# A windowed attention block on one core: the score correction moves from a stage of its own into the loop over columns

## What is computed

```
x = x + attention(layer_norm_over_channels(x))
t = tokens(x)                      # 1600 tokens of 128
t = t + mixture_of_experts(layer_norm(t))   # 8 experts, top 2, 128 -> 128 -> 128, gelu
```

```
qkv = xt @ w_qkv.T + b_qkv
q = q * 16 ** -0.5
k_w = unfold(k).reshape(B, K2, C, L)...     # the flat (channel, offset) axis read as (offset, channel)
attn = softmax(einsum('bhnc,bhnlc->bhnl', q, k_w)) * mask
out = einsum('bhnl,bhnlc->bhnc', attn, v_w);  out = out @ w_proj.T + b_proj
```

## Time and profile before

| | us |
|---|---|
| median of 3 runs | 521.09 |
| lowest, highest | 521.02, 524.63 |
| the profiled execution's own time | 524.98 |
| its span in the profile | 523.2 |

### The profile page before, as it was taken

The page is one execution under the profiler, slowest core; times in us unless marked ns, Lnnn a source line. Parts: engine busy times, 40 slices in busy tenths (PEclk is TensorE's granted clock), DMA queues, the critical chain, the costliest instruction groups (busy, mean ns, idle before and its releaser), DMA issues.

```text
span 523.2 us, 15325 instructions
## 1 busy us (share of the span) xinstructions
PE 482.3 (92%) x6330; PEld 333.3 (64%) x6330; DVE 344.0 (66%) x841; ACT 315.1 (60%) x479; POOL 228.8 (44%) x312
## 2 busy tenths in 40 slices
PE   4999986789769999999999999999869999998996
PEld 1799964555346777677777676777645545685553
DVE  1201387865029999999999888898567745553453
ACT  2390099992299999998999988798400000242442
POOL 9100000100019989989999899999150000000011
PEclk9775599965569999999999999999999955869999
DMA  5078007510102566656666544555864000004600
GB/s 187 16 227 235 7 2 208 198 76 23 63 38 94 191 217 192 223 189 199 204 203 205 199 169 163 172 176 186 210 225 86 1 0 0 1 1 151 246 16 31
DMA packets 27618, 68.40 MB, mean 131 GB/s; under 512 B 8037, under 2 KB 14966, under 8 KB 26494
## 3 DMA queue, kind: packets, MB, share of 16 engines
q1 hardware_dynamic: 26686, 66.03, 39.4%
q0 software_dynamic: 144, 1.18, 0.6%
q10 hardware_dynamic: 720, 0.23, 0.2%
HBM read 37.83 MB, written 28.47 MB: 127 GB/s over the span
## 4 chain that ended last, share of the span: by engine, by line
PE 80%; ACT 9%; issue 6%; POOL 2%; DVE 1%; DMA 1%; SPq 0%; POOLq 0%; ACTq 0%; DVEq 0%
PE ps L776 17%; PE ps L844 10%; PE ps L799 8%; PE ps L816 7%; ACT slabs L584 6%; PE ps L781 5%; PE ps L754 4%; PE ps L883 4%; PE ps L711 3%; PE ps L903 3%; PE ps L704 3%; PE ps L802 3%; PE ps L741 2%; PE ps L664 2%; PE ps L856 1%
## 5 line engine op out<-in xcount | busy, mean ns | idle before, releaser
L776 PE MATMUL ps<-slabs 128*32 128x401 f32 x528 | 116.6, 510 | 4.3 <-issue 4.1
L776 PE MATMUL ps<-prb,slabs 128*32 128x401 f32 x494 | 112.8, 513 | 0.0
L1028 DVE CUSTOM_DVE_ANT_0 scn<-ps,con 128x401 f32<-128x401 f32 x120 | 64.9, 563 | 20.3 <-PE ps L781 20.0
L610 ACT ACTIVATE exb<-scn,lowest 128x401 f32<-128x401 f32 x120 | 74.1, 620 | 5.5 <-DVE lowest L1028 5.0
L456 POOL TENSOR_TENSOR slabs<-con,qrot 128x192 f32<-128x192 f32 (+4 forms) x67 | 32.7, 492 | 100.2 <-DMA kimg<-qrot 75.1
L456 POOL TENSOR_TENSOR slabs<-con,kimg 128x192 f32<-128x192 f32 (+4 forms) x63 | 76.1, 1214 | 0.0
L781 PEld LDWEIGHTS ps<-con,slabs 128*32 128x32 f32 x960 | 42.0, 111 | 47.7 <-issue 47.3
L1018 DVE COPY_PREDICATED slabs<-con,zt 128x1152 f32<-128x1152 int32 x41 | 64.2, 1565 | 8.4 <-ACT slabs L577 8.3
L462 POOL TENSOR_TENSOR slabs<-con,sbd 128x384 f32<-128x384 f32 x40 | 43.2, 1080 | 49.2 <-ACT sbd L599 49.2
L507 POOL TENSOR_TENSOR xln<-xln,wide 128x400 f32<-128x400 f32 x4 | 4.9, 1230 | 129.9 <-DVE wide L1176 129.9
L781 PE MATMUL ps<-con,slabs 128*32 128x128 f32 x960 | 59.3, 276 | 0.0
(11 more groups left out here) (138 smaller groups left out, 849.0 us busy)
## 6 DMA issues: line engine op xcount, KB each, us to landing
slabs<-zsl SPq DMA_DIRECT2D x40, 539.5 KB, 4.4
zsl<-uv SPq DMA_DIRECT2D x44, 484.5 KB, 3.2
slabs<-combd SPq DMA_DIRECT2D x2, 1600.0 KB, 8.5
skb<-zsl SPq DMA_DIRECT2D x4, 539.5 KB, 7.0
kimd<-kimg SPq DMA_DIRECT2D x1, 1612.0 KB, 6.7
vimd<-vimg SPq DMA_DIRECT2D x1, 1612.0 KB, 9.6
frd<-wide SPq DMA_DIRECT2D x2, 800.0 KB, 6.6
con<-ctab POOLq DMA_DIRECT2D x1, 1155.5 KB, 5.6
```

The source lines that it names most:

```text
L610: nc.scalar.activation(v(ex[x & 1], a, (1, NC3)), v(scn, (x & 1) * NB * NC3 + a, (1, NC3)), ACT.Exp, scale=-1.0, bias=lowest[:, NB * (x & ...
L776: mm(bank(g, (1, NC3), parts=TW, p0=TW * i), w, v((kt, kh)[b & 1][x & 1], b // 2 * C, (1, NC3)), start=first, stop=False, skip_group_check ...
L1028: nc.vector.tensor_tensor_reduce(v(scn, i * NC3, (1, NC3)), bank(g, (1, NC3)), cv("pos"), 1.0, 3e38, ALU.add, ALU.min, lowest[:, i:i + 1]) ...
```

## The change

The score correction is computed per chunk of 4 columns x (XC = 4, ten chunks). Chunk 0 is computed in front of the loop by DVE, chunks 1 to 9 in it: POOL multiplies (`boundary_mul`), DVE adds (`boundary_add`), each a quarter of a chunk per iteration. PE and ACT have no part in it.

- The queries are projected once in plain layout (4 products of 400 columns, `qn`), written to DRAM (`qd`) and read back per chunk, spread over 120 rows (`q_load`: 4, 4, 4 and 3 transfers for the four groups of components).
- The key image goes to DRAM column by column with its border (`kx`, copied by DVE), and is read back in two parts (`edges_in`); DVE takes the differences (`edge_difference`).
- The crossing probabilities are now taken by PE (12 products of 32x46 per column in turn_probs, table `edge_y`); DVE multiplies them with a mask out of PSUM and adds two halves. `pick` and `boundary_probs` are gone.
- `mask` is computed only for the 16 columns of EDGES (240 columns of elements instead of 160); the other 24 use the row mask of the constants directly.
- In front of the loop zslab order is 0, 1, 2, 3; the loop starts when slabs 0 and 1 are turned; zturn(2) and (3) stand behind scores(0), zt_copy(2) and (3) behind half_blocks(1). `vimg` goes to DRAM after the loads of chunk 1.

```diff
+GROUPS = ((0, 4), (4, 8), (8, 12), (12, 15))
+EDGES = [x for x in range(SZ) if x < PAD or x >= SZ - PAD]
-        ZORDER = (1, 2, 3, 0)
+        ZORDER = (0, 1, 2, 3)
...
@@ sync
+            def q_load(c, g):
+                if c == 0:
+                    sp.wait_ge(S["qb_zero"], 1)
+                    sp.wait_ge(S["qn_out"], 16)
+                else:
+                    sp.wait_ge(S["kmul"], 4 * (c - 1) + g + 1)
+                for cc in range(*GROUPS[g]):
+                    n = NCC - cc
+                    sp.dma_start(v(qb, cc * XE, (1, XE), parts=8 * n),
+                                 dv(qd, cc * L + c * XE, (0, n), (HC * L, 8), (1, XE))).then_inc(q_in[g], 16)
...
             load(1)
+            for g in range(len(GROUPS)):
+                q_load(1, g)
+            sp.wait_ge(S["v_copied"], NQ)
+            images_out(sp, vimg, vimd, S["vim_out"])
             for i in range(SZ):
                 if i + 2 < SZ:
                     store(i + 2)
+                if i == 0:
+                    q_load(2, 0)
+                c, g = divmod(i + 9, XC)
+                if c < NXC:
+                    q_load(c, g)
                 if 2 <= i:
                     load(i)
@@ gpsimd
             def boundary(x):
+                pool.wait_ge(S["kadd"], x // XC + 1)
...
+            def boundary_mul(c, g):
+                a, z = GROUPS[g]
+                pool.wait_ge(q_in[g], 16 * (z - a) * (c + 1))
+                if g < 3:
+                    pool.wait_ge(S["kadd_sum"], 4 * (c - 1) + max(g, 1))
+                else:
+                    pool.wait_ge(S["kadd"], c)
+                n = 8 * NCC
+                gp.tensor_tensor(v(kprod, a * XE, (XE, z - a), (1, XE), parts=n), v(qb, a * XE, (XE, z - a), (1, XE), parts=n),
+                                 v(dkx, (c * XC + a) * SZ, (SZ, z - a), (1, XE), parts=n), ALU.mult).then_inc(S["kmul"], 1)
...
             for i in range(SZ + 2):
                 if 2 <= i + 1 < SZ:
                     spread(i + 1)
                     boundary(i + 1)
                 if 2 <= i < SZ:
                     mask(i)
-                if 0 <= i - 2 < SZ:
-                    pick(i - 2)
+                c, g = divmod(i + 6, XC)
+                if (c, g) > (1, 1) and c < NXC:
+                    boundary_mul(c, g)
@@ scalar
             half_blocks(0)
+            slab(0)
+            slab(1)
             half_blocks(1)
+            zt_copy(2)
+            zt_copy(3)
@@ tensor, turn_probs
+                for g in range(NB):
+                    for i in range(NTW):
+                        last = mm(bank(7, (64, 2), (1, NR), off=128 + HC * g + 1, parts=TW, p0=TW * i),
+                                  v(ex[x & 1], g * NC3 + TW * i, (1, TW)), cv("edge_y", (1, 2 * NR), off=2 * NR * i),
+                                  start=(g == 0), stop=(g == NB - 1), skip_group_check=True)
@@ vector
+            def boundary_add(c, g):
+                dve.wait_ge(S["kmul"], 4 * c + g + 1)
+                a, z = GROUPS[g]
+                row = lambda r, n=2: v(kprod, r * XE, (1, n * XE), parts=8 * NCC)
+                acc = lambda n=2, o=0: v(kacc, o * XE, (1, n * XE), parts=8 * NCC)
+                if g < 3:
+                    tt(row(a), row(a), row(a + 2), ALU.add).then_inc(S["kadd_part"], 1)
+                    if g:
+                        dve.wait_ge(S["kadd_part"], 3 * c + g + 1)
+                        if g > 1:
+                            dve.wait_ge(S["kadd_sum"], 4 * c + g - 1)
+                        elif c:
+                            dve.wait_ge(S["kadd"], c)
+                        tt(acc(), row(0) if g == 1 else acc(), row(a), ALU.add).then_inc(S["kadd_sum"], 1)
+                else:
+                    dve.wait_ge(S["kadd_sum"], 4 * c + 2)
+                    tt(acc(), acc(), row(a), ALU.add).then_inc(S["kadd_sum"], 1)
+                    dve.wait_ge(S["kadd_sum"], 4 * c + 3)
+                    tt(acc(1), acc(1), acc(1, 1), ALU.add).then_inc(S["kadd_sum"], 1)
+                    dve.wait_ge(S["kadd_sum"], 4 * c + 4)
+                    n = 8 * NCC
+                    tt(v(sbd, XC * c * YP + 7, (YP, XC), (1, SZ), parts=n), v(kacc, 0, (SZ, XC), (1, SZ), parts=n),
+                       v(kprod, (NCC - 1) * XE, (SZ, XC), (1, SZ), parts=n), ALU.add).then_inc(S["kadd"], 1)
...
             def weigh(x):
...
+                if x >= 1:
+                    dve.wait_ge(S["eb_red"], x)
+                tt(pb[:], bank(7, (64, 2), (1, SZ), off=128 + 8), mv(4 * SZ, (1, 2 * SZ)), ALU.mult).then_inc(S["pb_masked"], 1)
...
+                dve.wait_ge(S["pb_masked"], x + 1)
+                tt(v(ebd, x, (SZ, SZ)), v(pb, 0, (1, SZ)), v(pb, SZ, (1, SZ)), ALU.add).then_inc(S["eb_red"], 1)
...
                 if 0 <= i - 1 < SZ:
                     weigh(i - 1)
+                if i == 0:
+                    boundary_add(1, 0)
+                c, g = divmod(i + 5, XC)
+                if c < NXC:
+                    boundary_add(c, g)
```

More of the change, by code:

```diff
@@ L39 @@
 YP = SZ + 2 * 8 - 1
+NCC = HC - 1
 KH = SZ + 8
@@ L45 @@
 NSPLIT = 4
-NCC = HC - 1
+KIMX = PS * (PS + 1)
+NX = SZ + NCC - 1
+GX = NX * (PS + 1)
+GX0 = 21
+XC = 4
+NXC = SZ // XC
+XE = XC * SZ
+GROUPS = ((0, 4), (4, 8), (8, 12), (12, 15))
 GIMG = (SZ - 1) * PS + SZ + NCC
@@ L91, in consts @@
     inside = lambda d: (y[None, None] + d[:, :, None] >= 0) & (y[None, None] + d[:, :, None] < SZ)
-    t["rm"], t["cm"] = inside(dy), inside(dx)
-    hot = (hs[:, None] == np.arange(8)[None]) & (r[:, None] != 0)
-    t["hot"] = hot
-    t["hot_rev"] = hot[:, ::-1]
+    first, second = (hs % 2 == 1) & (r != 0), (hs % 2 == 0) & (r != 0)
+    rows = inside(dy)
+    t["rm"] = np.concatenate([rows, rows[:, :1] * first[:, None, None], rows[:, :1] * second[:, None, None]], 1)
+    t["cm"] = np.concatenate([inside(dx), inside(dx)[:, :1], inside(dx)[:, :1]], 1)
+    t["hot_of"] = (p % 8)[:, None] == np.arange(8)[None]
+    yy = np.arange(NR)[None] == (p // 8 + p % 8)[:, None]
+    t["edge_y"] = np.stack([yy & (p % 8 == a)[:, None] for a in range(8)], 1)
     j = np.arange(NPS)[None, None] + TS * (p[:, None, None] // TW)
@@ L198, in program @@
         pm = [sb(f"pm{i}", PN) for i in range(2)]
-        mx = [sb(f"mx{i}", 4 * SZ) for i in range(2)]
-        hotp = [sb(f"hotp{i}", 8 * SZ) for i in range(2)]
+        mx = [sb(f"mx{i}", 6 * SZ) for i in range(2)]
+        pb = sb("pb", 2 * SZ)
         osel = sb("osel", NPS * SZ)
@@ L286, in images_in, with edges_in @@
                           dv(d, K + 1 - HC, (IMGP + 1, NCC), (HC * IMGP, 8), (1, GIMG))).then_inc(done, 16)
+        def edges_in(eng, part):
+            a, n = ((0, GX0), (GX0, NX - GX0))[part]
+            for dst, row in zip(gk[part], (2 * HC + 1, 0)):
+                eng.dma_start(v(dst, 0, (1, n * (PS + 1)), parts=8 * NCC),
+                              dv(kimd, row * KIMX + (K + 1 - HC + a) * (PS + 1), (KIMX + PS + 1, NCC), (HC * KIMX, 8),
+                                 (1, n * (PS + 1)))).then_inc(gk_in[part], 16)
         def live(cc):
@@ L558, in _ @@
             zslab(0)
-            for k in range(NQ):
-                act.wait_ge(S["qt_ready"], k + 1)
-                nc.scalar.activation(v(ex[k // 2], (k % 2) * 4 * C, (1, 4 * C), parts=TT),
-                                     bank(4 + k, (1, 4 * C), parts=TT), ACT.Copy).then_inc(S["qt_copied"], 1)
+            zslab(1)
             image(vimg, 1, "v_ready", "v_copied")
-            zslab(1)
             act.wait_ge(S["v_copied"], NQ)
-            act.wait_ge(S["qt_copied"], NQ)
+            zslab(2)
+            zslab(3)
             def zt_copy(n):
@@ L690, in _ @@
             pe.wait_ge(S["w_q"], 80)
-            for t in range(NT):
-                last = mm(bank(4 + t // 4, (1, C), off=C * (t % 4), parts=TT), xln[:, t * TT:(t + 1) * TT], wqr[:],
-                          start=True, stop=True, skip_group_check=True)
-                if t % 4 == 3:
-                    last.then_inc(S["qt_ready"], 1)
+            for k in range(NQ):
+                mm(bank(4 + k, (1, Q)), wqr[:], xln[:, k * Q:(k + 1) * Q], start=True, stop=True).then_inc(S["qn_ready"], 1)
             for k in range(NQ):
@@ L827, in _ @@
                     scores(i)
+                if i == 0:
+                    zturn(2)
+                    zturn(3)
+                    pe.wait_ge(S["zt_copied"], 3 * NZK)
                 if 0 <= i - 1 < SZ:
```

287 lines of the change are left out of this document (120 added, 167 removed).

## The result

The changed kernel takes 506.25 us (median of 4 runs, 503.0 to 508.43); the kernel before took 522.86 us beside it (4 runs). The ratio is 0.9675, with a 95% interval of 0.9597 to 0.9754: faster by 3.3%. The forecast was 502 us. The profiled execution took 504.65 us, its span 502.9; the sum had given 504.3 for the span. Medians and ratios leave out a run that lies over 1.5% above the fastest of its kernel; that is one run in this document, 499.85 us of the three edits together.

What follows compares the result with a forecast made beforehand. It saw the score correction ahead of the loop as the stage to remove, all four engines nearly full in the loop; 523.2 - 70.5 - 2.4 + 54 = 504.3 us of span, hence 502 us, range 460 to 522.

Steps and rivals of the forecast that it cites:

- The start: Ahead of the loop: scores(0) at 75 instead of 150.6, scores(2) at 90.1 instead of 160.61, 70.5 us gained.
- The term for SP: At the start, POOL's chunk 1 products wait for 15 transfers that SP issues at about 0.35 us each behind load(1).
- The loop on PE: In turn_probs, 12 more products (24 instructions) per x add 0.42 us, bounds 0.2 and 0.9.
- The loop on DVE and POOL: In the loop, DVE's additions and POOL's products hold each other up: 7.04 us per x, 1.65 more than 5.39.
- no wait at all: In the loop, the bound where DVE's additions and POOL's products do not hold each other up.
- a wait for each: In the loop, the bound where every DVE addition collides with POOL's reading operations; the forecast took this.
- The first rival: In the loop, additions do not collide: 5.95 us per x, later 6.5, 19 us given back, time 467; chance 0.2.
- From x = 24 on: Loop, x = 24 to 34: POOL has more bands, 7.35 us per x against 6.08, 14 us given back.
- the 54 given back: Whole loop: 36 and 2 us for x = 2 to 23, 14 for 24 to 34, 2 for 35 to 39.
- The end: After the loop: edge sums no longer need POOL, first tail product about 384.3 on the old scale, 2.4 us gained.
- Slower (531): In the loop, POOL's product goes ahead of DVE's additions every iteration: 7.9 to 8.2 us per x, 531 us; chance 0.13.
- The late start (514): At the start, chunk 1's loads stand late on SP and PE waits: 12 us less gained, 514 us; chance 0.12.

Runs made afterwards that it cites:

- the three edits together: Changed kernel with POOL's chunk products in halves, the value-image difference in pieces of 448 columns, and query copies and loads earlier in SP's queue: 492.48 us (5 runs).
- the repeat: The changed kernel measured once more with nothing altered: 505.08 us (6 runs), ratio 0.9667 to the kernel before.
- the doubled products: Changed kernel with PE's 12 edge products per column made twice (24 more instructions): 504.36 us.
- the fills: Changed kernel with every POOL product in the loop (bands, boundary, chunk) replaced by fills that read nothing: 475.07 us (4 runs), ratio 0.9088.
- the product between bands and boundary: Changed kernel with POOL's in-loop product of the correction placed between spread and boundary instead of behind boundary and mask: 501.24 us.
- pieces of 448 columns: Changed kernel with POOL's difference of the value images taken in five pieces instead of one operation: 497.23 us.
- halves: Changed kernel with POOL's in-loop product of the correction made in two operations of 320 (or 320 and 160) columns: 499.59 us.

## Why the prediction was right

**The start** was forecast at 75 and 90.1 for scores(0) and scores(2), and came at 73.00 and 91.03. Errors cancelled here. The rotated queries were ready at 57.5 instead of 62.3. Some 2 us of that are the new query products, which run in less time than those they replace. The other 3 belong to this execution: PE's granted clock was at 2.4 GHz from 31 to 34 us (1.00), while in the repeat it was mostly at 1.2 GHz there (0.63 in the mean); its products L742 have a median of 414 ns instead of 283, and its queries came at 60.6. The forecast let chunk 0 decide, done at 74. It was done at 67.6, and the copies decided: they took 11.0 us where 6.5 was taken, outside the bounds of 5 and 9. The term for SP, 0.35 us per load, was mis-sized too: fifteen took 11.61 us, 0.77 each. The first product of chunk 1 needs the first four of them and started at 80.82, the third at 86.02. These products stand ahead of the third band product on POOL, and took back what scores(0) had won.

**The loop on PE**: 0.42 us per x was too much. The periods without additions say 0.23 (6.31 - 6.08), the doubled products 0.25, just inside the lower bound.

**The loop on DVE and POOL** was right in its mechanism and in size: 7.04 us per x forecast, 7.04 measured. The detail holds as well: POOL waits for chunk c ahead of boundary(4c) (7.12 us of idle time at 156.62), and the turn behind it is held for about 0.6 us, as worked out. The four iterations from 158.44 on, by the starts of the turns, took 7.93, 7.23, 6.41 and 6.18 us, where 8.1, 7.8, 6.05 and 6.2 were worked out. So the order of the waits is right, and that the mean agrees to the last digit is luck. The choice between "no wait at all" and "a wait for each", on which 35 us hung (502 against 467), is settled by the fills: with none of POOL's readers in the loop the time is 475.07. The first rival's 467 was 8 us too low, though, so the exclusion is worth at most 30 us, not 35.

What the forecast drew from the Trainium skill, page "SBUF — State Buffer", section "SBUF: two separate sides" (a VectorE operation with two SBUF inputs excludes a GpSimd operation that reads SBUF, for the whole instruction) is borne out. These traces agree, also in the clause on reading: a fill by GpSimd, which reads nothing, left a turn at 1.50 us, and beside a product of the same places one took 2.12; with fills alone in the loop the longest of 41 turns took 1.577 us, in the changed kernel 2.661.

From x = 24 on the forecast was 7.35 per x. Two groups of four there, 243.05 to 298.16 in the chain, took 55.1 us, 6.89 per x, so some 5 us of the 54 given back were not needed. From scores(2) to the first tail product 47.6 us came back, against 51.6 by the forecast's terms.

**The end** is the step that failed in sign. It gave 2.4 us gained, because edge sums no longer need POOL. They do not need its result, but the sum in its new form reads two tensors in SBUF and meets POOL's 4.92 us difference: from the difference's start to the first tail product it takes 9.23 us, where the earlier trace rows had 7.56. The working had found the rule for the turn and the additions, had counted the edge sum among the operations under it, and did not apply it to the one long instruction of POOL at the end. Eleven of the thirteen kernels have the difference in one piece. In ten of them an edge sum started behind it and took 2.7 to 5.0 us; in the eleventh, the product between bands and boundary, the sum started ahead of it and took 0.22, and the step from the difference's start to the first tail product took 7.74 us. By that kernel the wait cost 1.5 of the 9.23 us, and without it there would still have been no gain of 2.4. How much of the wait pieces of 448 columns save is not shown, since in both kernels that have them the sum missed it by its moment.

**The rivals.** Slower (531) needed POOL ahead of DVE in every iteration; the stall ahead of boundary(4c) prevents that, and the turns in between take 1.50 to 1.52 us, their own length. The late start (514) came halfway: SP's loads were late as it said, but scores(2) were within a us.

The sum was good to 1.4 us of span, and that is in part luck: 70.5 for 69.6, in which errors of 3 to 6 us cancel, 51.6 for 47.6, and 0 for the tail's 1.7, which the repeat (136.5) shows to be scatter. From span to time the forecast went by the kernel before, whose profiled execution lay 3.9 us above its median; this one's lies 1.6 below its own. That makes 502 out of 504.3 and puts it 4 us under the 506.25 measured, or 3 under the repeat's 505.08. The gain between medians was forecast as 18.9 and measured as 16.6.

## What to carry over

Before work is moved onto DVE and GpSimd side by side, list on each the instructions by what they read in SBUF: here turns, additions and edge sums, all with two SBUF inputs, waited out the reading instruction of GpSimd that they met, and the price was what was left of GpSimd's instruction, not the length of DVE's. So shorten those first: halves gave 8.0 us of loop here, another order 2.6. And look for the one long instruction outside the loop, since the same happens there.

## What was not expected of the hardware

- A fill by GpSimd beside DVE's copy_predicated left it at 1.50 us, its length alone; a product of GpSimd of like length made it 2.12.
- DVE's additions of 16 columns (L1020), 0.154 us at the shortest, had a mean of 0.704 us beside GpSimd's products.
- A small load issued by SP took 0.77 to 0.88 us of SP's queue each (fifteen in 11.61 us at 74.83, and in 13.26 us at 44.42).
- Two copies of the queries by DMA took 10.7 to 11.0 us from issue to use where SP issued them 0.9 to 1.4 us behind two slab stores, and 7.4 to 8.9 where it issued them 2.7 to 3.5 us behind.
